# A four-layer attention and mixture-of-experts block on one core: what the two result accumulators start from, how tokens are numbered, and who copies the padding row numbers

## The reference, cut to what matters

```python
x = x + tanh(g_xattn[0]) * attention(layernorm(x), ctx)         # step 1
x = x + tanh(g_ffn[0])   * ternary_mlp(layernorm(x))            # step 2
x = x + tanh(g_xattn[1]) * long_conv(ctx, layernorm(x))         # step 3
h = layernorm(x)                                                # step 4
w, ids = top_k(softmax(h @ gate_w.T), 6);  w = w / sum(w)
comb = zeros((2048, 64));  comb[token, ids] += w
routed = einsum(silu(h @ Wg[e]) * (h @ Wu[e]) * comb[:, e], W_down[e])   # summed over e
shared = (silu(h @ Sg) * (h @ Su)) @ S_down
x = x + tanh(g_ffn[1]) * (routed + shared)
```

## Time and profile before

| what | us |
|---|---|
| median of 3 runs | 808.74 |
| lowest, highest | 807.09, 811.56 |
| span of the profiled execution, first to last instruction | 809.0 |
| busy in it: PE, DVE, POOL, ACT | 660.4, 483.3, 448.0, 293.8 |

### The profile page before, as it was taken

The page is one execution under the profiler, slowest core; times in us unless marked ns, Lnnn a source line. Parts: engine busy times, 40 slices in busy tenths (PEclk is TensorE's granted clock), DMA queues, the critical chain, the costliest instruction groups (busy, mean ns, idle before and its releaser), DMA issues.

```text
span 809.0 us, 12013 instructions
## 1 busy us (share of the span) xinstructions
PE 660.4 (82%) x3068; PEld 501.3 (62%) x3068; DVE 483.3 (60%) x1590; ACT 293.8 (36%) x641; POOL 448.0 (55%) x481
## 2 busy tenths in 40 slices
PE   3688984764998767988887659999999999999930
PEld 2354542433887646766666548888888888888720
DVE  3887776997687777777773615445434543454322
ACT  2146666864344423444433212323332333233200
POOL 2577877120344313766666614676776677667752
PEclk9699998887999978999999789999999999999975
DMA  6347545586888664545425266999999999999587
GB/s 226 123 134 249 199 156 208 171 279 237 290 316 304 229 209 140 193 162 183 173 94 200 92 218 174 241 242 237 260 250 230 234 258 254 231 240 233 88 178 227
DMA packets 94691, 169.07 MB, mean 209 GB/s; under 512 B 10944, under 2 KB 60032, under 8 KB 94656
## 3 DMA queue, kind: packets, MB, share of 16 engines
q1 hardware_dynamic: 70368, 137.05, 50.6%
q0 software_dynamic: 23424, 30.70, 20.6%
q10 hardware_dynamic: 864, 0.93, 0.3%
HBM read 94.30 MB, written 74.33 MB: 208 GB/s over the span
## 4 chain that ended last, share of the span: by engine, by line
PE 55%; DVE 17%; issue 9%; POOL 7%; DMA 5%; ACT 2%; another core or an unknown queue 2%; DVEq 1%; SPq 1%; POOLq 0%; ACTq 0%
PE psum L1027 13%; PE psum L1040 7%; PE psum L1031 7%; PE psum L798 5%; PE psum L874 5%; POOL xs_rows L694 5%; PE psum L1045 4%; PE psum L1015 4%; DVE hh L1573 2%; PE psum L953 2%; PE psum L770 2%; PE psum L865 2%; PE psum L780 1%; DMA acc<-hh,toki 1%
## 5 line engine op out<-in xcount | busy, mean ns | idle before, releaser
L731 POOL DMA_INDIRECT acc<-hh,toki x128 | 198.8, 1553 | 101.5 <-DVE hh L1868 62.3
L1868 DVE TENSOR_SCALAR hh<-psum,wtok 128x256 f32<-128x256 f32 x128 | 56.0, 480 | 155.8 <-DMA acc<-hh,toki 98.7
L694 POOL DMA_INDIRECT xs_rows<-Z,slot x96 | 96.6, 1006 | 58.4 <-DVE slot L1749 32.4
L1027 PE MATMUL psum<-qT,Z 128*128 128x256 f32 x512 | 122.7, 383 | 3.5 <-DVE hh L1858 3.5
L1027 PEld LDWEIGHTS psum<-qT,Z 128*128 128x128 f32 x512 | 93.1, 192 | 14.5 <-issue 4.4
L618 POOL TENSOR_TENSOR rstd<-mv,neghalf 128x1 f32<-128x1 f32 (+1 forms) x48 | 36.7, 765 | 75.1 <-DVE mv L1364 75.1
L1298 ACT ACTIVATE qT<-psum 128x512 f32<-128x512 f32 x64 | 38.2, 598 | 102.2 <-PE psum L1015 100.3
L798 PE MATMUL psum<-wt,hTs 128*128 128x512 f32 x128 | 61.8, 627 | 9.4 <-ACT hTs L1122 9.4
L1031 PE MATMUL psum<-qT,Z 128*112 128x256 f32 x256 | 66.6, 383 | 0.0
L1040 PE MATMUL psum<-Z,hh 128*128 128x256 f32 x256 | 61.0, 381 | 1.2 <-DVE hh L1858 1.2
L953 PE MATMUL psum<-qT,wt 128*128 128x256 f32 (+1 forms) x192 | 51.4, 424 | 8.9 <-DVE H L1754 8.9
(11 more groups left out here) (316 smaller groups left out, 1253.6 us busy)
## 6 DMA issues: line engine op xcount, KB each, us to landing
Z<-in_wexp SPq DMA_DIRECT2D x66, 496.0 KB
xs_rows<-fill SPq DMA_DIRECT2D x64, 272.0 KB, 3.3
Z<-xs_rows SPq DMA_DIRECT2D x64, 272.0 KB
kv_rows<-Z SPq DMA_DIRECT2D x12, 688.0 KB, 3.8
kvb<-kv_rows SPq DMA_DIRECT2D x8, 688.0 KB
Z<-co_rows SPq DMA_DIRECT2D x8, 688.0 KB
Z<-kv_rows SPq DMA_DIRECT2D x8, 688.0 KB
acc<-fill SPq DMA_DIRECT2D x4, 1024.0 KB, 8.9
```

The costliest lines, as they stand in the source:

```text
L694: pool.indirect_dma_start(out=xs_rows[:, :], out_offset=bass.IndirectOffsetOnAxis(ap=slot[:, t, k:k + 1], axis=0), in_=H[:, t, :], in_offs ...
L731: pool.indirect_dma_start(out=acc[s % 2][:, :], out_offset=bass.IndirectOffsetOnAxis(ap=toki[:, g, j:j + 1], axis=0), in_=y_sb[:, s, j, :] ...
L1027: m = pe.matmul(pA[par][:, g * CAP:(g + 1) * CAP], wgu_sb[:, s, k, g * P:(g + 1) * P], xT[:, par, k, :], start=(k == 0), stop=(k == 1))
L1868: m = dve.tensor_scalar(y_sb[:, s, j, :], pY[par][:, j * D:(j + 1) * D], wtok[:, g, j:j + 1], None, ALU.mult)
```

## The change

The accumulators are no longer set to zero. SP copies the rows of `X` after step 3 into `acc[0]` (`seed_rows`, 16 transfers of 128 KB) and the gated shared result into `acc[1]` (`seed_base`, 16 of 128 KB), as they come out, in its queue behind the loads of the routing stage. The tokens are numbered by their output row, so that accumulators and output have the same order; the end reads and stores runs of 4 rows (4 KB) a partition, and `back[0] + back[1]` is the output. `X` is not read any more at the end, `shared_add` is gone, and so are POOL's two additions. POOL copies `gcol` itself, DVE has no part in the padding, and SP waits for `padded` before the overflow blocks. ACT (before its first expert) and POOL (before its first add) wait for all seeds. The zero fill of the 256 dump rows stays.

```diff
-                        for c in range(T // P // 8):
-                            sp.dma_start(a_[8 * c * P:8 * (c + 1) * P, :].rearrange("(p r) d -> p r d", r=8),
-                                           fill[:, 0:1, 0:D].to_broadcast([P, 8, D])).then_inc(filled, 16)
+            def seed_rows(u):
+                sp.wait_ge(x3_done, u + 1)
+                for t in range(2 * u, 2 * u + 2):
+                    sp.dma_start(acc_heads[0][t], X[:, t, :]).then_inc(seeded, 16)
+
+            def seed_base(w):
+                sp.wait_ge(base_ready, w + 1)
+                for q in range(2):
+                    sp.dma_start(acc_heads[1][2 * w + q], base[:, w, q * D:(q + 1) * D]).then_inc(seeded, 16)
...
+                if i >= 2:
+                    seed_rows(i - 2)
+                if i >= 4:
+                    seed_base(i - 4)
...
+            seed_base(NPAIR - 4)
+            seed_rows(NPAIR - 2)
+            seed_base(NPAIR - 3)
             sp.wait_ge(o3_ready, NH)
+            seed_rows(NPAIR - 1)
+            seed_base(NPAIR - 2)
             for s in range(4):
                 load_weights(s, s, w_in[s])
+            seed_base(NPAIR - 1)
             sp.wait_ge(scattered, 16 * NT * K)
...
+            sp.wait_ge(padded, 32 * n)
+            alone(sp, "sp")
             with sp.Fori(0, n) as b:
...
-                             acc[1][c * 4 * P:(c + 1) * 4 * P, :].rearrange("(t p) d -> p t d", p=P)).then_inc(early_in[c], 16)
+                sp.dma_start(back[1][:, 4 * c:4 * c + 4, :], acc_lines[1][:, 4 * c:4 * c + 4, :]).then_inc(early_in[c], 16)
...
+                sp.dma_start(back[0][:, 4 * c:4 * c + 4, :], acc_lines[0][:, 4 * c:4 * c + 4, :]).then_inc(back_in[c], 16)
             for c in range(4):
-                for t in range(4 * c, 4 * c + 4):
-                    sp.dma_start(out.rearrange("b (h j) d -> h b j d", j=HD)[t], X[:, t, :]).then_inc(rows_out, 16)
+                sp.wait_ge(sum_done, c + 1)
+                sp.dma_start(out_lines[:, 4 * c:4 * c + 4, :], back[0][:, 4 * c:4 * c + 4, :]).then_inc(rows_out, 16)
...
-            pool.iota(H[:, :, CT:CT + 1], pattern=[[P, NT], [0, 1]], base=0, channel_multiplier=1, allow_small_or_imprecise_dtypes=True)
+            pool.iota(H[:, :, CT:CT + 1], pattern=[[HD, NT], [0, 1]], base=0, channel_multiplier=1,
+                      allow_small_or_imprecise_dtypes=True).then_inc(c_done, 1)
+            pool.wait_ge(c_done, 2)
+            pool.tensor_scalar(H[:, :, CT], H[:, :, CT], row_f[:, 0:1], None, ALU.add)
...
             with pool.Fori(0, n) as b:
+                pool.tensor_copy(gcol[:, :], gidx[:, bass.ds(2 * b, 2)]).then_inc(gcol_ready, 1)
                 pool.wait_ge(gcol_ready, b + 1)
...
+            pool.wait_ge(seeded, 16 * 2 * NT)
...
-            pool.tensor_tensor(X[:, 12:16, :], X[:, 12:16, :], back[0][:, 12:16, :], ALU.add).then_inc(sum3_step, 1)
...
-            act.wait_ge(x_full, 2)
+            act.wait_ge(seeded, 16 * 2 * NT)
...
             dve.wait_ge(consts, 1)
+            link(dve.tensor_copy(pid_i[:, 0:1], pid[:, :]))
+            link(dve.tensor_scalar(pid_i[:, 1:2], pid_i[:, 0:1], 3, None, ALU.logical_shift_right))
+            dve.tensor_scalar(row_f[:, :], pid_i[:, 1:2], float(NT * HD - HD), None, ALU.mult)
...
-            shared_add(0)
-            shared_add(1)
             shared_hidden(NPAIR - 1, 2)
...
-            with dve.Fori(0, n) as b:
-                dve.tensor_copy(gcol[:, :], gidx[:, bass.ds(2 * b, 2)]).then_inc(gcol_ready, 1)
-                dve.wait_ge(padded, 32 * b + 32)
-                alone(dve, "dve")
...
-            for c in range(3):
+            for c in range(4):
                 dve.wait_ge(early_in[c], 16)
                 dve.wait_ge(back_in[c], 16)
-                dve.tensor_tensor(xc, xc, back[0][:, 4 * c:4 * c + 4, :], ALU.add).then_inc(sum_done, 1)
+                rows = back[0][:, 4 * c:4 * c + 4, :]
+                dve.tensor_tensor(rows, rows, back[1][:, 4 * c:4 * c + 4, :], ALU.add).then_inc(sum_done, 1)
```

More of the change, by code:

```diff
@@ L69, in build @@
     x_rows = nc.dram_tensor("x_rows", (T, D), f32, kind="Internal").ap()
+    acc_heads = [a_[0:T, :].rearrange("(b h j) d -> h b j d", h=NH, j=HD) for a_ in acc]
+    acc_lines = [a_[0:T, :].rearrange("(p r) d -> p r d", r=NT) for a_ in acc]
+    out_lines = out.rearrange("b l d -> (b l) d").rearrange("(p r) d -> p r d", r=NT)
     with ExitStack() as ctx:
@@ L185, in build @@
         dump = sb("dump", [P, 1])
+        pid_i = sb("pid_i", [P, 2], i32)
+        row_f = sb("row_f", [P, 1])
         lg = sb("lg", [P, 2, 2, E])
@@ L315, in build @@
         sy_done = sem("sy_done")
-        base_ready, x_full = sem("base_ready"), sem("x_full")
+        base_ready, seeded = sem("base_ready"), sem("seeded")
         xT_full = sem("xT_full")
@@ L346, in build @@
         sum_done = sem("sum_done")
-        sum3_step = sem("sum3_step")
         early_in = [sem(f"early_in{c}") for c in range(4)]
@@ L567, in _ @@
             for c in range(4):
-                sp.dma_start(back[0][:, 4 * c:4 * c + 4, :],
-                             acc[0][c * 4 * P:(c + 1) * 4 * P, :].rearrange("(t p) d -> p t d", p=P)).then_inc(back_in[c], 16)
+                sp.dma_start(back[0][:, 4 * c:4 * c + 4, :], acc_lines[0][:, 4 * c:4 * c + 4, :]).then_inc(back_in[c], 16)
             for c in range(4):
[L571 to L574, removed]
-                for t in range(4 * c, 4 * c + 4):
-                    sp.dma_start(out.rearrange("b (h j) d -> h b j d", j=HD)[t], X[:, t, :]).then_inc(rows_out, 16)
-            sp.wait_ge(rows_out, 2 * 16 * NT)
+                sp.wait_ge(sum_done, c + 1)
+                sp.dma_start(out_lines[:, 4 * c:4 * c + 4, :], back[0][:, 4 * c:4 * c + 4, :]).then_inc(rows_out, 16)
+            sp.wait_ge(rows_out, 16 * (NT + 4))
         @block.gpsimd
@@ L584, in _ @@
             pool.memset(eps2[:, 1:2], 1e-5)
+            pool.iota(pid[:, :], pattern=[[0, 1]], base=0, channel_multiplier=1, allow_small_or_imprecise_dtypes=True)
             pool.memset(neghalf[:, :], -0.5).then_inc(p_step, 1)
@@ L609, in _ @@
                                base=0, pattern=[[1, E]], channel_multiplier=-1)
-            for t_, base, pat, cm in ((iota_e, 0, [[1, E]], 0), (iota_row, 1, [[T, E]], 0), (pid, 0, [[0, 1]], 1),
+            for t_, base, pat, cm in ((iota_e, 0, [[1, E]], 0), (iota_row, 1, [[T, E]], 0),
                                       (dump, E * T, [[0, 1]], 1)):
@@ L1754, in shared_hidden @@
                 dve.tensor_tensor(shid[0:fw, par, c], ssil[0:fw, par, c], s_up[c][0:fw, CAP:2 * CAP], ALU.mult).then_inc(shid_ready, 1)
-            def shared_add(w):
-                dve.wait_ge(base_ready, w + 1)
-                x = X[:, 2 * w:2 * w + 2, :].rearrange("p t d -> p (t d)")
-                dve.tensor_tensor(x, x, base[:, w], ALU.add).then_inc(x_full, 1)
             diag(0)
-            dve.wait_ge(c_done, 2)
+            dve.wait_ge(c_done, 3)
             dve.wait_ge(qT_ready, NT)
@@ L1872, in _ @@
                 weights(0, g)
-                if g >= 2:
-                    shared_add(g)
                 if g >= 1:
@@ L1911, in _ @@
                     dve.tensor_scalar(y_sb[:, j, 0, :], pY[j][:, 0:D], wtok[:, j, 0:1], None, ALU.mult).then_inc(o_yr, 1)
-            for c in range(3):
+            for c in range(4):
                 dve.wait_ge(early_in[c], 16)
-                xc = X[:, 4 * c:4 * c + 4, :]
-                m = dve.tensor_tensor(xc, xc, back[1][:, 4 * c:4 * c + 4, :], ALU.add)
-            link(m)
-            for c in range(3):
-                xc = X[:, 4 * c:4 * c + 4, :]
                 dve.wait_ge(back_in[c], 16)
-                dve.tensor_tensor(xc, xc, back[0][:, 4 * c:4 * c + 4, :], ALU.add).then_inc(sum_done, 1)
+                rows = back[0][:, 4 * c:4 * c + 4, :]
+                dve.tensor_tensor(rows, rows, back[1][:, 4 * c:4 * c + 4, :], ALU.add).then_inc(sum_done, 1)
 def kernel(**inputs):
```

3 lines of the change are left out of this document (1 added, 2 removed).

## The result

The changed kernel takes 802.94 us in the median of five executions (800.98 to 807.51), the kernel before 811.24 beside it (807.09 to 814.60). The prediction was 799.7 us, 0.9888 of the 808.74 that it started from, with a range of 796.5 to 804.0.

What follows compares the result with a forecast made beforehand. PE was taken to bound the expert stage, so an earlier start moves all of it. 809.0 - 5.3 (padding and clock) - 3.7 (end) = 800.0 profiled, 799.7 median; range 796.5 to 804.0, the forecast's own 797.5 to 801.2.

Steps and rivals of the forecast that it cites:

- Padding off DVE: Start of expert stage: PE's 3.50 us wait for DVE's `expert_hidden`, held by the padding transfers, goes.
- The slow clock behind it: PE's work after that wait runs at granted clock 0.50; without idle time 1.76 us gained, bounds 0 and 1.76.
- Rival A: PE's clock falls near the expert stage's start even without a gap, leaving 3.5 us there: 801.5 us; chance 0.11.
- The end: After the last overflow add: four stores replace 16 and DVE's addition replaces POOL's; 3.7 us gained, bounds 2 to 5.
- Seeds, fills, additions: Seed transfers in the routing stage, dropped zero fills and early additions: 0 us each; seeds bounded by 0 and 1.
- rival E: Late seeds hold ACT's first expert; with 4 us over, 803.7 us; chance 0.06 together with unnamed losses.
- Rival B: End gains only about 1.7 us, as longer pieces delay POOL's second overflow add or stores stay slow: 801.7; chance 0.14.
- Rival C: Expert stage really bound by DMA, so the 5.3 us are lost: 805.0, no measurable change; chance 0.06.
- Rival D: POOL's adds land later with the new row order; beyond 7.15 us, each us costs about 31 over 31 pairs; chance 0.06.

Runs made afterwards that it cites:

- the first profile: Changed kernel, profiled execution of the first result, slowest of five: span 805.8 us; a later profile of the same kernel, the second, has 799.3.
- the filler run with 16 matmuls: Kernel before, padding hold kept, plus 16 matmuls with unused results ahead of PE's third `up`: 812.07 us, ratio 1.0024.

## Why the prediction was right

**Padding off DVE (3.50 forecast).** Shown. The wait is gone in each profile without the hold, and the part alone, clock included, gave 4.9 us by the ratio (4.4 by the medians) where 5.3 was the term.

**The slow clock behind it (1.76).** Shown. 7.24 us became 5.48 with the hold gone, and also with the hold kept and PE occupied. Rival A is out: with no idle time the clock did not fall. But I took one trace for the rule. In two of the four profiles with the hold the clock did not fall behind the wait, which was shorter there, and the hold cost 3.1 and 1.8 us; the two in which it fell, 5.4 and 5.5. So the full 5.3 is what the hold costs in some executions, and that the medians gave nearly that much is in part luck. Nor had I counted that the stage's start has a slow spell of its own, of varying length: in the first profile it ended some 3.5 us later than before, and of the 5.3 us only 4.1 are left there (15.75 against 19.85); in the second it is 5.5.

**The end (3.7, bounds 2 to 5).** 4.3 and 4.1 us in the two profiles, 17.6 to 13.3 or 13.5, with 14 forecast. The 512 KB store landed in 3.7 to 3.9 us, as the nearest row, 3.8, said. The estimate of 3.2 from the Trainium skill ("DMA: Bandwidth & Descriptors", the anatomy of one DMA) was 0.5 too small for it, and the row was the better guide; the page gives that fit for transfers that GpSimd issues, and these are SyncE's, so it was also taken past what it states. The step was short in one reason: I set the 16 stores against four by their number, and the larger half of the gain is that plain rows are issued faster, 0.49 us against 0.65.

**Seeds, fills, additions (0).** Shown together, to within about a microsecond: seeds without the new row order gave 789.66 where the padding part alone gave 789.00. In the first profile `seed_base` 7 stood in SP's queue until 467.83, and the rows of the first experts were requested 2.89 us behind the last scatter, not 2.45; rival E is there with 0.4 us, and it decides nothing. In five of the seven profiles with seeds the distance is the old 2.45.

**Rival B.** Not seen: from the second overflow add to the read it is 7.9 us in one profile and 6.7 in the other, 7.5 before. That part alone varies (3.9 to 8.0 over all profiles), so take both adds together, from the first to the read: 11.3 to 12.4 us in the six profiles with 4 KB pieces, 10.6 to 12.5 in the seven with 1 KB pieces. The rule of the Trainium skill ("DMA: Bandwidth & Descriptors", queues, rings and completion order) that each DMA engine takes turns among its queues packet by packet would have longer pieces delay the add; with 4 KB pieces beside it, no delay shows.

**Rival C.** Out: each microsecond that the third `up` gained was still there at the last transposes (264.09 against 264.08).

**Rival D.** Its mechanism, adds waiting for their own landings, does occur: 57.2 and 55.7 us in two of the six profiles with seeds and the new row order, and 0.8 to 4.6 in the other four. In all seven profiles that lack one of the two it is 1.2 to 8.6. The pair of experts stays at 9.00 us all the same. The one pair of 9.84 us in the first profile is a wait of PE for a load of rows, and the filler run with 16 matmuls, whose adds waited 7.5 us, has one of 9.64 for the same reason, while the profile with 55.7 us of waits has none over 9.04; so that pair isn't shown to be the adds' doing. What the waits go with is a lag. From about the eighth expert to the last two pairs POOL starts the adds of an expert, in the median, 4.0 us (first of a pair) and 7.3 us (second) behind DVE's result in these two profiles, and 0.9 and 2.6 us in all eleven others. The cost shows at the end: with 1.3 us of the lag left, POOL waits 3.40 and 3.72 us for a landing ahead of the last pair's adds, and the first overflow add comes 27.3 and 27.6 us behind the last transposes, against 22.9 to 25.1 in the eleven others. I had put the price in the pair, times 31, and no price on the tail, where POOL's delay has no PE work to hide behind. The median landing, on which the rival's limit of 7.15 us rested, doesn't tell the two apart either: 5.7 and 5.6 us there, but also 5.6 and 5.5 in profiles with 4.5 and 0.8 us of waits. The row order alone doesn't bring it about (3.9 us), and neither do the seeds alone (3.4). Whether the two together do, in some executions, or whether such executions come in any kernel here and didn't fall among the seven, the runs don't settle. The tail accounts for 4.3 us of the 6.5 between the spans of the two profiles.

**The number.** The first result is 3.2 us above the forecast, inside the range but above the forecast's own 797.5 to 801.2. It lies nearer to the 801.5 and 801.7 of rivals A and B, and neither of those happened. The kernel before, too, is 2.5 above its earlier median there (811.24 against 808.74). The difference is 8.3 us where 9.0 was forecast, and in the two other comparisons 8.8 (793.42 - 784.63) and 9.2 (809.00 - 799.84). By the ratios it is 0.9908, 0.9881 and 0.9869 where 0.9888 was forecast. In single profiles the parts don't add up so neatly: 3.2 and 9.7 us of span, since the tail and the stage's start, both priced at nothing, move by several us between executions.

Two slips in the prediction's working change nothing. The forecast's own range, by the terms that it names (an end of 5 to 2, a microsecond of spread), is 797.4 to 802.4, not 797.5 to 801.2. And PE's run of nines starts in the 25th slice, not the 26th, and the last but one still has three tenths.

## What to carry to other kernels

A wait that leaves TensorE idle for a few microseconds can cost more than its length, because the work behind it may run at the lower clock; price the stretch up to the next mark that repeats in the steady part, not the wait alone, and read it in more than one execution before you count it in full. When results leave through many small transfers, look first at how long the queue's engine takes to issue each, and at whether another numbering of the rows makes the pattern plain: where the rows are written by index, the order alone showed no cost here. And price an engine's backlog at the end of a stage separately from its pace within the stage.

## What the hardware showed that I had not expected

- The same hold costs 5.4 us in one execution and 1.8 or 3.1 in another: a clock that is still low ahead of it makes TensorE arrive later, and behind waits of 1.58 and 2.85 us the clock stayed at full speed, where it fell behind 3.50 and 3.62.
- SP's time to issue a 128 KB store depends on the pattern: 0.65 us for groups of 8 adjacent rows with a jump behind each group, 0.49 for rows at one even stride, and reads of the same size through the view by heads 0.63 (10.15/16). A store of 512 KB in pieces of 4 KB took 0.34, less than any of them.
- One kernel, two executions: POOL's indirect adds of 128 rows waited 57.2 us for their own landings in one and 2.2 in the other, with median landings of 5.7 and 5.2 us. In the first it ran 4.0 and 7.3 us behind VectorE's results (medians by place in the pair) through most of the stage, in the second 0.9 and 2.6. What starts that is open.
